# A Mamba-style block with a gated feed-forward: first batch's opening spread over other engines, and the batch loop written out

## The chip, the core and the metric

The kernel runs on one core of a Trainium2 chip. Its engines work side by side, each from its own instruction queue: TensorE (PE; its weight loads are shown as PEld), VectorE (DVE), ScalarE (ACT), GpSimd (POOL), and SyncE (SP), which here only issues DMA transfers. They are ordered by semaphores alone. The metric is the device time of one execution in microseconds, the median of several runs; lower is better.

## The reference

Input x is 4 x 512 x 512 (batch, position, channel), all in fp32. With D = 1024, N = 16, R = 32:

```python
xn = (x - mean) / sqrt(var + 1e-5)
u, gate = split(xn @ W_in.T)                     # 1024 each
u = silu(causal_conv4(u) + conv_b)               # depthwise, along the positions
dt, Bm, Cm = split(u @ Wx.T, [32, 48])           # 32, 16, 16
dt, Bm, Cm = rmsnorm(dt)*w1, rmsnorm(Bm)*w2, rmsnorm(Cm)*w3
delta = softplus(dt @ Wdt.T + dt_bias)
# for every position t:
state = exp(delta_t * A) * state + (delta_t * u_t) * B_t
y_t = sum_n state * C_t
s = ((y + u * D_param) * silu(gate)) @ W_out.T
ffn = (silu(xn @ w_gate.T) * (xn @ w_up.T)) @ w_down.T   # inner width 1376
out = x + s * silu(ffn)
```

## The kernel before

Channels lie on the 128 partitions and the 512 positions along a row, so the recurrence over positions is VectorE's scan instruction on a 128 x 512 tile, one for each of 8 channel tiles and 16 states: 128 scans a batch, in 64 slots of two. A slot s of a batch is: ScalarE makes two decay tiles `exp(delta * A)` in the PSUM banks `dA[0]`, `dA[1]` (L598); GpSimd makes the input pair `dBu = v * B` with v = delta * u, 128 x 1024, in one of three buffers (L814); VectorE scans twice (L1041); TensorE transposes the states into the banks `hT` (L1391); and VectorE (L970, L961), or ScalarE with GpSimd (L694, L784), adds them times C to `yT`. Around that, in every slot, each engine has further steps written out by slot number (`side(s)`): the feed-forward of the same batch, whose weight products are TensorE's largest work, and the opening of the next batch (normalisation, u, gate, delta). Matmuls on x are done in three products of high and low parts (`from_x`, L1102, 12 matmuls for a tile); the low part of a weight entry is the rest that GpSimd takes (`rest_w`, L750) after ScalarE's rounding (`round_w`, L463). Entries come through a ring of two.

The first batch has no batch before it, so its opening stands ahead of all slots:

- SyncE loads x in four tiles and the first weight entries (two at once, each later one when GpSimd has taken the rest of the one two before). ScalarE's queue issues the identity and seven constants (L444, L445); semaphore `const_in` counts the seven.
- VectorE takes `bn_stats` of the four tiles (L878). GpSimd's `power_ln` (L719 to L736) turns them to scale and shift in eleven small steps of 4 columns, one the power -0.5 (L732). ScalarE normalises (L459), TensorE transposes, ScalarE and VectorE split x in high and low (L453, L882). Ahead of that VectorE waits for all constants and halves two of them (L933, L934).
- u in 8 tiles: TensorE; ScalarE's first tap (L492); VectorE's three taps (L892); ScalarE's tanh (L499) and "+1" (L503); GpSimd's product (L755). Then TensorE's small matmuls with Wx (L1107), two groups of four for each u tile.
- ScalarE squares, VectorE sums rows (L903, L904), GpSimd's `power_rms` scales, adds and takes the power over 12 columns (L741 to L745), ScalarE scales rows (L518, L519); dt and B are transposed, B goes out to DRAM and comes back row by row, spread over the partitions (`bb`).
- delta in two pairs of tiles: TensorE (L1120), ScalarE's exponentials (L581) and logarithms (L548), for which it loads another function table, VectorE's clamp (L945), GpSimd's v (L766). Then ScalarE loads the first table again (for tanh, L552), takes the second of the first four gate tiles and the C rows (L526), VectorE copies C (L909) and makes the products of gate tiles 0 and 1 (L913). Gate tiles 2 and 3 wait on TensorE for the banks of 0 and 1.
- Slot 1's ScalarE part ends with the rounding of the first feed-forward entry, which needs all four gate tiles; GpSimd takes its rest in slot 2, and TensorE's feed-forward starts on it.

`sequences` runs the body of a batch for batch 0, for batches 1 and 2 in a hardware loop with the batch number in a register, and for batch 3.

## Time and profile before

| | |
|---|---|
| median of 3 runs | 1177.55 us (1175.94 to 1177.86) |
| the profiled execution | 1172.87 us, span 1171.1 us |
| TensorE busy | 1062.0 us, 91% |
| VectorE busy | 1035.4 us, 88% |
| GpSimd busy | 998.4 us, 85% |
| ScalarE busy | 702.6 us, 60% |
| granted TensorE clock, mean | 0.968 of full |

The span goes from the first to the last instruction of the profiled execution; its own time has 1.8 us around it. Busy shares are means over stages that have different limits, so they do not tell what an edit is worth; the waits at the place of the edit do. A granted clock of 1.0 is 2.4 GHz, of 0.5 it is 1.2 GHz.

### The profile page before, as it was taken

Reading aid. Unit: us, or ns where it says so; the run is one execution under the profiler, and the core shown is the slowest. Engines: PE = TensorE matmul, PEld = TensorE weight load, DVE = VectorE, ACT = ScalarE, POOL = GpSimd, SP = SyncE. Lnnn points to the kernel's source line nnn. Section 1 sums busy time; section 2 is a strip of 40 time slices with the busy share of each in tenths; the row PEclk is TensorE's granted clock in tenths of the full one; section 3 lists DMA queues with packets and bytes.
Section 4 is the critical chain, followed back from the end, with each engine's and each line's share of the span. In section 5 each row is a group of like instructions: output and inputs, shape, how many; then the busy total and the mean of one; then the engine's idle time right before and its main releaser. Section 6 shows DMA issues by size and latency. Waiting matters only on the chain.

```text
span 1171.1 us, 16696 instructions
## 1 busy us (share of the span) xinstructions
PE 1062.0 (91%) x5072; PEld 757.3 (65%) x5072; DVE 1035.4 (88%) x1232; ACT 702.6 (60%) x1140; POOL 998.4 (85%) x572
## 2 busy tenths in 40 slices
PE   5979988889989999989997999998998999999767
PEld 4757766666658776666756786576756787555444
DVE  4469999999989999899987999899998999888895
ACT  4656646866665756677573766476576665465440
POOL 3678899899988899789987899879989889879961
PEclk9969999899999999999998999999999999999878
DMA  4636754534333544343323453334233353325310
GB/s 129 215 107 225 233 193 142 171 118 135 101 98 137 209 144 161 127 153 100 115 76 128 153 208 145 117 135 153 89 111 118 135 181 108 126 99 180 117 63 37
DMA packets 46567, 160.83 MB, mean 137 GB/s; under 512 B 5355, under 2 KB 5611, under 8 KB 37004
## 3 DMA queue, kind: packets, MB, share of 16 engines
q1 hardware_dynamic: 45424, 159.14, 39.6%
q8 instruction: 44, 0.72, 0.2%
q10 hardware_dynamic: 1052, 0.59, 0.2%
q14 instruction: 47, 0.39, 0.1%
HBM read 135.33 MB, written 24.38 MB: 136 GB/s over the span
## 4 chain that ended last, share of the span: by engine, by line
PE 52%; DVE 20%; issue 12%; POOL 11%; ACT 4%; DVEq 1%; DMA 0%; SPq 0%; POOLq 0%; ACTq 0%
PE pj L1102 18%; PE hT L1391 11%; DVE sb_h L1041 10%; PE pj L1300 7%; POOL sb_dBu L814 5%; DVE sb_yT L970 5%; PE pj L1334 5%; PE pj L1365 3%; PE pj L1120 2%; DVE sb_un L892 2%; PE pj L1409 2%; PE pj L1107 2%; POOL sb_yT L784 2%; POOL sb_un L755 1%; POOL sb_v L766 1%
## 5 line engine op out<-in xcount | busy, mean ns | idle before, releaser
L814 POOL TENSOR_TENSOR sb_dBu<-sb_v,sb_bb 128x1024 f32<-128x1024 f32 x256 | 607.1, 2385 | 28.5 <-DVE sb_h L1041 20.0
L1041 DVE TENSOR_TENSOR_SCAN sb_h<-dA,sb_dBu 128x512 f32<-128x512 f32 x512 | 597.9, 1212 | 29.0 <-POOL sb_dBu L814 17.0
L598 ACT ACTIVATE dA<-sb_delta,sb_apar 128x512 f32<-128x512 f32 x512 | 345.7, 688 | 246.1 <-DVE sb_h L1041 242.4
L1102 PE MATMUL pj<-sb_x_hi,sb_w_sp 128*128 128x512 f32 x1208 | 344.3, 409 | 21.8 <-DVE sb_un L892 12.0
L1391 PE MATMUL hT<-sb_ident,sb_h 128*128 128x128 f32 x2048 | 287.3, 282 | 63.8 <-DVE sb_yT L970 50.3
L1391 PEld LDWEIGHTS hT<-sb_ident,sb_h 128*128 128x128 f32 x2048 | 242.3, 144 | 148.6 <-issue 50.2
L970 DVE SCALAR_TENSOR_TENSOR sb_yT<-hT,sb_cs,sb_yT 128x512 f32<-128x512 f32 x335 | 239.3, 740 | 43.8 <-PE hT L1391 43.2
L1102 PEld LDWEIGHTS pj<-sb_x_hi,sb_w_sp 128*128 128x128 f32 x1208 | 220.6, 192 | 84.6 <-issue 24.3
L784 POOL TENSOR_TENSOR sb_yT<-sb_yT,sb_part 128x512 f32<-128x512 f32 x141 | 181.2, 1285 | 57.6 <-ACT sb_part L694 57.4
L694 ACT ACTIVATE sb_part<-hT,sb_cs_act 128x512 f32<-128x512 f32 x141 | 96.4, 684 | 139.6 <-PE hT L1391 138.0
L1102 PE MATMUL pj<-sb_x_lo,sb_w_sp 128*128 128x512 f32 x604 | 167.1, 400 | 0.0
L1102 PEld LDWEIGHTS pj<-sb_x_lo,sb_w_sp 128*128 128x128 f32 x604 | 116.2, 192 | 27.1
L1334 PE MATMUL pj<-sb_S,sb_ring 128*128 128x512 f32 x264 | 121.8, 599 | 0.0
L1300 PE MATMUL pj<-sb_u,sb_ring 128*128 128x512 f32 x192 | 86.6, 594 | 0.0
L1334 PEld LDWEIGHTS pj<-sb_S,sb_ring 128*128 128x128 f32 x264 | 46.9, 190 | 52.6 <-issue 52.6
L892 DVE SCALAR_TENSOR_TENSOR sb_un<-pj,sb_cw,sb_un 128x511 f32<-128x511 f32 (+2 forms) x93 | 69.5, 748 | 4.8 <-ACT sb_un L492 2.6
L750 POOL TENSOR_TENSOR sb_w_sp<-sb_ring,sb_w_sp 128x1024 fp32r<-128x1024 f32 x21 | 50.0, 2382 | 27.0 <-ACT sb_w_sp L463 26.9
L1300 PEld LDWEIGHTS pj<-sb_u,sb_ring 128*128 128x128 f32 x192 | 34.6, 190 | 34.9 <-issue 34.6
L770 POOL TENSOR_TENSOR sb_u<-sb_u,sb_sgate 128x512 f32<-128x512 f32 x32 | 41.2, 1293 | 11.3 <-DVE sb_u L919 11.3
L766 POOL TENSOR_TENSOR sb_v<-sb_delta,sb_un 128x1024 f32<-128x1024 f32 x16 | 38.3, 2392 | 8.9 <-DVE sb_delta L945 8.5
L761 POOL TENSOR_TENSOR sb_delta<-sb_delta,sb_v 128x1024 f32<-128x1024 f32 x14 | 33.5, 2390 | 11.1 <-ACT sb_v L548 11.1
L755 POOL TENSOR_TENSOR sb_un<-sb_v,sb_un 128x512 f32<-128x512 f32 x32 | 41.1, 1291 | 0.0
(126 smaller groups left out, 800.0 us busy)
## 6 DMA issues: line engine op xcount, KB each, us to landing
sb_w_sp<-w_cache SPq DMA_DIRECT2D x55, 1024.0 KB, 4.8
sb_ring<-w_ring SPq DMA_DIRECT2D x67, 512.0 KB, 3.4
sb_bb<-b_rows SPq DMA_DIRECT2D x128, 256.0 KB, 3.6
w_cache<-sb_w_sp SPq DMA_DIRECT2D x19, 1024.0 KB, 4.9
sb_xio<-x SPq DMA_DIRECT2D x7, 1024.0 KB, 8.0
out<-sb_xio SPq DMA_DIRECT2D x3, 1024.0 KB, 5.7
sb_xio<-x SPq DMA_DIRECT2D x4, 256.0 KB, 3.5
out<-sb_xio SPq DMA_DIRECT2D x4, 256.0 KB, 2.0
```

What stands on the lines that cost most here:

```text
L598: nc.scalar.activation(dA[g % 2][:, :], delta[:, j, :], ACT.Exp, scale=apar[:, j, n:n + 1]).then_inc(dA_done, 1)
L694: nc.scalar.activation(dst, hT[c % H_BANKS][:, :], ACT.Copy, scale=cs_act[:, c, n:n + 1]).then_inc(ev_done, 1)
L755: nc.gpsimd.tensor_tensor(un[:, j, :], cth[:, j % 2, :], un[:, j, :], ALU.mult).then_inc(u_done, 1)
L784: nc.gpsimd.tensor_tensor(y, y, part[:, (len(acts) - q) % 2, :], ALU.add).then_inc(yp_done, 1)
L814: nc.gpsimd.tensor_tensor(dBu[:, dbu_buffer(s), :, :], v[:, j:j + 2, :], bb[:, i % B_RING, :].unsqueeze(1).to_broadcast([P, 2, T]), ALU.mu ...
L892: nc.vector.scalar_tensor_tensor(out=acc[:, k:T], in0=bank[:, 0:T - k], scalar=cw[:, j, KC - 1 - k:KC - k], in1=acc[:, k:T], op0=ALU.mult, ...
L970: nc.vector.scalar_tensor_tensor(out=y, in0=hT[c % H_BANKS][:, :], scalar=cn, in1=y, op0=ALU.mult, op1=ALU.add).then_inc(y_done, 1)
L1041: nc.vector.tensor_tensor_scan(h[:, i % 2, 2 * part + e, :], dA[g % 2][:, :], dBu[:, dbu_buffer(s), e, :], 0.0, ALU.mult, ALU.add).then_in ...
L1102: done = nc.tensor.matmul(bank[:, :], w[:, kk * P:(kk + 1) * P], xs[:, kk, :], start=(p == 0), stop=(p == len(products) - 1))
L1300: done = nc.tensor.matmul(pj[e % 2][:, :], ring[:, slot_of(b, OUT0 + e), part, m * P:(m + 1) * P], u[:, j, :], start=(j == 0), stop=(j == ...
L1334: done = nc.tensor.matmul(pj[DOWN_BANK[e]][:, :], ring[:, slot_of(b, DOWN0 + x3 // 2), x3 % 2, t % 4 * P:(t % 4 + 1) * P], S[:, t, :], sta ...
L1391: done = nc.tensor.transpose(hT[c % H_BANKS][:, j * P:(j + 1) * P], h[:, i % 2, j, c * P:(c + 1) * P], ident[:, :])
```

## The change

- **Constants.** The seven constant transfers move from ScalarE's queue to SyncE's, between the first and the second weight entry.
- **Layer statistics.** VectorE does the small steps (the sum of means is scaled by an immediate, scale and shift are reordered so that the doubling falls away); GpSimd keeps the power alone.
- **u.** For the last two of eight tiles VectorE does "+1" and product in one instruction; ScalarE's "+1" and GpSimd's product fall away.
- **RMS.** VectorE does scale and add; GpSimd's power is split in one over eight columns (dt and B) and one over four (C), each with its own count, so that `rms_done` has two counts for batch 0.
- **v and dBu of slots 0 and 1** are made by VectorE, in `first_pair`, behind the clamp of their pair, with a semaphore of their own (`dBu_first`); counts of `dBu_done` are two lower from there on (`pairs_made`).
- **Decays of slot 0** come on ScalarE ahead of the second pair's logarithms. Its second gate tanh and the C rows move into slot 0's side work; VectorE's first gate product moves ahead of the pairs, the second into slot 0, the copy of C into slot 1.
- **The loop.** `sequences` is a Python loop over four batches, so all of them are written out with constant counts.

```diff
@@ -325,14 +326,16 @@
...
+        def pairs_made(b, s):
+
+            return dBu_done, b * SLOTS + s - 2
+
...
-        def sequences(eng, body):
-            body(0, True, False)
-            with eng.Fori(1, NB - 1) as b:
-                body(b, False, False)
-            body(NB - 1, False, True)
+        def sequences(body):
+            for b in range(NB):
+                body(b, b == 0, b == NB - 1)
@@ -356,6 +359,10 @@
...
                 load(p % W_RING, (FIRST + RING_FIRST)[p])
+                if p == 0:
+                    for dst, src in consts:
+                        sp.dma_start(dst[:], src).then_inc(const_in, 16)
+                    sp.dma_start(lnw[:, :], ln_w.partition_broadcast(P)).then_inc(const_in, 16)
@@ -407,7 +414,10 @@
...
                     if what == "row":
-                        sp.wait_ge(dBu_done, b * SLOTS + 2 * k + 2)
+                        if first and k == 0:
+                            sp.wait_ge(dBu_first, 2)
+                        else:
+                            sp.wait_ge(*pairs_made(b, 2 * k + 2))
@@ -440,9 +450,6 @@
...
             act.dma_start(ident[:, :], ident_d).then_inc(id_in, 16)
-            for dst, src in consts:
-                act.dma_start(dst[:], src).then_inc(const_in, 16)
-            act.dma_start(lnw[:, :], ln_w.partition_broadcast(P)).then_inc(const_in, 16)
@@ -512,7 +519,7 @@
...
-                act.wait_ge(rms_done, c + 1)
+                act.wait_ge(rms_done, 1 if isinstance(c, int) and c == 0 else c + 2)
@@ -559,6 +566,7 @@
...
             act.wait_ge(half_done, 2)
+            act.wait_ge(init_done, N_INIT)
@@ -566,8 +574,8 @@
...
                     conv_tanh(0, j - 1)
-                    conv_plus1(0, j - 1)
-            act.wait_ge(init_done, N_INIT)
+                    if j - 1 < KD - 2:
+                        conv_plus1(0, j - 1)
@@ -579,11 +587,13 @@
...
                     nc.scalar.activation(delta[:, j, :], first_z_bank[j][:, :], ACT.Exp).then_inc(ze_done, 1)
+                if p == 1:
+
+                    act.wait_ge(del_done, 1)
+                    for e in range(2):
+                        nc.scalar.activation(dA[e][:, :], delta[:, e, :], ACT.Exp, scale=apar[:, e, 0:1]).then_inc(dA_done, 1)
...
                     softplus_log(0, j, delta)
-            gate_tanh(0, 1, pj[1])
-
-            take_c(0)
@@ -601,6 +611,10 @@
...
                 def side(s):
+                    if first and s == 0:
+                        gate_tanh(0, 1, pj[1])
+                        act.wait_ge(rms_done, 2)
+                        take_c(0)
@@ -612,7 +626,7 @@
...
                         if j == JH and not first:
-                            act.wait_ge(dBu_done, b * SLOTS)
+                            act.wait_ge(*pairs_made(b, 0))
@@ -694,7 +708,8 @@
...
                 for s in range(SLOTS):
-                    decay(s)
+                    if not (first and s == 0):
+                        decay(s)
@@ -751,7 +766,8 @@
...
             def conv_silu(c, j):
-                pool.wait_ge(th1_done, c * KD + j + 1)
+
+                pool.wait_ge(th1_done, c * KD + j + 1 if isinstance(c, int) and c == 0 else c * KD + j - 1)
@@ -783,16 +799,21 @@
...
-            power_ln(0)
+            pool.wait_ge(ln_var, 1)
+            nc.gpsimd.tensor_tensor(rstd[:, 1, :], rstd[:, 0, :], half[:, 0:TC], ALU.pow).then_inc(ln_rstd, 1)
...
                     rest_w(p % W_RING, p % HI_RING, p + 1)
-                conv_silu(0, j)
-            power_rms(0)
-            inputs(0, 0)
+                if j < KD - 2:
+                    conv_silu(0, j)
+
+            pool.wait_ge(mse_done, 2)
+            nc.gpsimd.tensor_tensor(ms[:, 2, :, 0:2], ms[:, 1, :, 0:2], half[:, 0:2 * TC].rearrange("p (c g) -> p c g", g=2),
+                                    ALU.pow).then_inc(rms_done, 1)
+            nc.gpsimd.tensor_tensor(ms[:, 2, :, 2:3], ms[:, 1, :, 2:3], half[:, 0:TC].unsqueeze(2), ALU.pow).then_inc(rms_done, 1)
@@ -805,6 +826,11 @@
...
                             pool.wait_ge(out_dma, b * 16)
+                    if first and s < 2:
+
+                        continue
+                    if first and s < 4:
+                        pool.wait_ge(v_done, s - 1)
@@ -814,8 +840,6 @@
...
                                             ALU.mult).then_inc(dBu_done, 1)
-                    if s == 0 and first:
-                        inputs(b, 1)
@@ -929,6 +953,19 @@
...
                 ln_stats(0, t)
+            dve.wait_ge(ln_stat, TC)
+            nc.vector.tensor_tensor(mv[:, 0, :], stats[:, :, 1], stats[:, :, 4], ALU.add).then_inc(ln_aggr, 1)
+            nc.vector.tensor_tensor(mv[:, 1, :], stats[:, :, 1], stats[:, :, 4], ALU.subtract).then_inc(ln_aggr, 1)
+            nc.vector.tensor_tensor(mv[:, 2, :], stats[:, :, 2], stats[:, :, 5], ALU.add).then_inc(ln_aggr, 1)
+            dve.wait_ge(ln_aggr, 3)
+            nc.vector.tensor_scalar(mv[:, 0, :], mv[:, 0, :], -0.5, None, ALU.mult).then_inc(ln_aggr, 1)
+            nc.vector.tensor_tensor(mv[:, 1, :], mv[:, 1, :], mv[:, 1, :], ALU.mult).then_inc(ln_aggr, 1)
+            nc.vector.tensor_scalar(mv[:, 2, :], mv[:, 2, :], 1.0 / H, LN_EPS, ALU.mult, ALU.add).then_inc(ln_aggr, 1)
+            dve.wait_ge(ln_aggr, 6)
+            nc.vector.scalar_tensor_tensor(out=rstd[:, 0, :], in0=mv[:, 1, :], scalar=0.25, in1=mv[:, 2, :],
+                                           op0=ALU.mult, op1=ALU.add).then_inc(ln_var, 3)
+            dve.wait_ge(ln_rstd, 1)
+            nc.vector.tensor_tensor(rstd[:, 2, :], mv[:, 0, :], rstd[:, 1, :], ALU.mult).then_inc(ln_rstd, 1)
@@ -937,18 +974,35 @@
...
                 taps(0, j, first_u_bank[j])
+            for j in (KD - 2, KD - 1):
+                dve.wait_ge(th_done, j + 1)
+                dve.wait_ge(u_done, j)
+                nc.vector.scalar_tensor_tensor(out=un[:, j, :], in0=cth[:, j % 2, :], scalar=1.0, in1=un[:, j, :],
+                                               op0=ALU.add, op1=ALU.mult).then_inc(u_done, 1)
             rms_squares(0)
+            dve.wait_ge(ms_done, 2)
+            nc.vector.tensor_scalar(ms[:, 1, :, 0:1], ms[:, 0, :, 0:1], 1.0 / R, RMS_EPS, ALU.mult, ALU.add).then_inc(mse_done, 1)
+            nc.vector.tensor_scalar(ms[:, 1, :, 1:3], ms[:, 0, :, 1:3], 1.0 / N, RMS_EPS, ALU.mult, ALU.add).then_inc(mse_done, 1)
...
                 weigh(slice(t, t + 1), first_ssm_bank[t][:, 0:F].unsqueeze(1))
-            for j in range(JH):
-                dve.wait_ge(sp_done, j + 1)
-                step = nc.vector.scalar_tensor_tensor(out=delta[:, j, :], in0=delta[:, j, :], scalar=Z_MAX, in1=first_z_bank[j][:, :],
-                                                      op0=ALU.min, op1=ALU.max)
-                if j % 2 == 1:
-                    step.then_inc(del_done, 1)
-            hand_c(0)
-            for j in range(2):
-                gate_silu(0, j, pj[j])
+            gate_silu(0, 0, pj[0])
+
+            def first_pair(p):
+                pair = slice(2 * p, 2 * p + 2)
+                for j in (2 * p, 2 * p + 1):
+                    dve.wait_ge(sp_done, j + 1)
+                    step = nc.vector.scalar_tensor_tensor(out=delta[:, j, :], in0=delta[:, j, :], scalar=Z_MAX, in1=first_z_bank[j][:, :],
+                                                          op0=ALU.min, op1=ALU.max)
+                step.then_inc(del_done, 1)
+                dve.wait_ge(del_done, p + 1)
+                nc.vector.tensor_tensor(v[:, pair, :], delta[:, pair, :], un[:, pair, :], ALU.mult).then_inc(v_done, 1)
+                if p == 0:
+                    dve.wait_ge(b_in[0], 16)
+                dve.wait_ge(v_done, p + 1)
+                nc.vector.tensor_tensor(dBu[:, dbu_buffer(p), :, :], v[:, pair, :], bb[:, 0, :].unsqueeze(1).to_broadcast([P, 2, T]),
+                                        ALU.mult).then_inc(dBu_first, 1)
+
+            first_pair(0)
@@ -973,6 +1027,10 @@
...
                 def side(s):
+                    if first and s == 0:
+                        gate_silu(0, 1, pj[1])
+                    if first and s == 1:
+                        hand_c(0)
@@ -1034,7 +1092,12 @@
...
                     i, part = s // 2, s % 2
-                    dve.wait_ge(dBu_done, b * SLOTS + s + 1)
+                    if first and s < 2:
+                        if s == 1:
+                            first_pair(1)
+                        dve.wait_ge(dBu_first, s + 1)
+                    else:
+                        dve.wait_ge(*pairs_made(b, s + 1))
```

(Lines that only pass the changed arguments of `sequences` are left out.)

## Rows read from the trace of the kernel before

**Rows 1.** The page, chain that ended last: share of the span by engine.
```profile
PE 52%; DVE 20%; issue 12%; POOL 11%; ACT 4%; DVEq 1%; DMA 0%; SPq 0%; POOLq 0%; ACTq 0%
```
**Rows 2.** Timeline, start: start us, us, engine, line, operation, out<-in, count [idle before <-releaser].
```profile
4.41 0.99 ACTq L445 DMA_DIRECT2D sb_lnw<-ln_w  x1
...
5.40 0.69 DVE L878 BATCH_NORM_STATS2 sb_stats<-sb_xio 128x6 f32<-128x512 f32 x1 [0.24 <-DMA sb_xio<-x]
...
7.81 0.69 DVE L878 BATCH_NORM_STATS2 sb_stats<-sb_xio 128x6 f32<-128x512 f32 x1 [1.71 <-DMA sb_xio<-x]
...
10.38 1.02 POOL L732 TENSOR_TENSOR sb_rstd<-sb_mv,sb_half 128x4 f32<-128x4 f32 x1
...
11.63 0.18 DVE L933 TENSOR_SCALAR sb_cw<-sb_cw 128x32 f32<-128x32 f32 x1 [3.12 <-DMA sb_lnw<-ln_w]
...
12.00 2.93 ACT L459 ACTIVATE sb_xio<-sb_xio,sb_rstd 128x512 f32<-128x512 f32 x4 [5.29 <-POOL sb_rstd L736]
...
17.32 2.48 DVE L882 TENSOR_TENSOR sb_x_lo<-pj,sb_x_hi 128x512 fp32r<-128x512 f32 x4 [5.44 <-ACT sb_x_hi L453]
```
**Rows 3.** Timeline, end of the stage that makes u.
```profile
41.01 2.32 DVE L892 SCALAR_TENSOR_TENSOR sb_un<-pj,sb_cw,sb_un 128x511 f32<-128x511 f32 x3 [0.32 <-ACT sb_un L492]
...
44.31 2.48 POOL L755 TENSOR_TENSOR sb_un<-sb_v,sb_un 128x512 f32<-128x512 f32 x2
...
44.85 0.61 PE L1107 MATMUL dA<-sb_wx,sb_un 128*128 128x64 f32 x4
...
47.34 0.61 PE L1107 MATMUL dA<-sb_wx,sb_un 128*128 128x64 f32 x4
```
**Rows 4.** Timeline, row sums of squares to their powers.
```profile
49.67 0.21 POOL L741 TENSOR_TENSOR sb_ms<-sb_ms,sb_per 128x12 f32<-128x12 f32 x1 [2.88 <-DVE sb_ms L904]
...
50.26 2.27 POOL L745 TENSOR_TENSOR sb_ms<-sb_ms,sb_half 128x12 f32<-128x12 f32 x1
```
**Rows 5.** Timeline, softplus to the first slots.
```profile
61.01 2.34 POOL L766 TENSOR_TENSOR sb_v<-sb_delta,sb_un 128x1024 f32<-128x1024 f32 x1 [8.47 <-DVE sb_delta L945]
...
63.56 1.28 ACT L552 ACT_TABLE_LOAD   x1
...
66.26 1.30 ACT L598 ACTIVATE dA<-sb_delta,sb_apar 128x512 f32<-128x512 f32 x2
...
66.40 1.27 DVE L913 SCALAR_TENSOR_TENSOR sb_sgate<-sb_sgate,pj 128x512 f32<-128x512 f32 x2
...
74.98 0.60 ACT L552 ACTIVATE sb_sgate<-pj 128x512 f32<-128x512 f32 x1 [0.93 <-PE pj L1102]
...
81.35 2.34 DVE L1041 TENSOR_TENSOR_SCAN sb_h<-dA,sb_dBu 128x512 f32<-128x512 f32 x2
```
**Rows 6.** The chain in order of time: start us, us, engine, tile, line, count.
```profile
21.12 19.05 PE pj L1102 x84
...
79.00 5.49 PE pj L1102 x12
...
625.87 4.33 issue
...
631.31 4.41 PE pj L1102 x12
...
637.03 2.75 PE pj L1102 x12
```
**Rows 7.** Timeline: first scan of batches 1 to 3, third step-size addition of 2, 3.
```profile
346.78 1.23 DVE L1041 TENSOR_TENSOR_SCAN sb_h<-dA,sb_dBu 128x512 f32<-128x512 f32 x1 [2.54 <-POOL sb_dBu L814]
...
617.79 1.22 DVE L1041 TENSOR_TENSOR_SCAN sb_h<-dA,sb_dBu 128x512 f32<-128x512 f32 x1 [2.61 <-POOL sb_dBu L814]
...
677.93 2.38 POOL L761 TENSOR_TENSOR sb_delta<-sb_delta,sb_v 128x1024 f32<-128x1024 f32 x1
...
894.64 1.22 DVE L1041 TENSOR_TENSOR_SCAN sb_h<-dA,sb_dBu 128x512 f32<-128x512 f32 x1 [2.52 <-POOL sb_dBu L814]
...
948.59 2.38 POOL L761 TENSOR_TENSOR sb_delta<-sb_delta,sb_v 128x1024 f32<-128x1024 f32 x1
```

More of the change, by code:

```diff
@@ L259, in build @@
         dA_done = sem("dA_done")
+        dBu_first = sem("dBu_first")
         dBu_done = sem("dBu_done")
@@ L432, in sequence @@
                         sp.dma_start(xio[:, :, :], rows(x, b)).then_inc(xr_in, 16)
-            sequences(sp, sequence)
+            sequences(sequence)
             for c in range(TC):
@@ L708, in sequence @@
                         round_entry(b, *HI_AT[s])
-            sequences(act, sequence)
+            sequences(sequence)
         @block.gpsimd
@@ L851, in sequence @@
                         inputs(b + 1, s - SLOTS + 2)
-            sequences(pool, sequence)
+            sequences(sequence)
             for m, c in OFF_ADDS[False]:
@@ L1048, in sequence @@
                     side(s)
-            sequences(dve, sequence)
+            sequences(sequence)
             b = NB - 1
@@ L1411, in tail_out @@
                     done.then_inc(tail_ps, 1)
-            sequences(pe, sequence)
+            sequences(sequence)
             b = NB - 1
```

## The prediction

> **What bounds the kernel now.** I read the chain that ended last first [rows 1]: TensorE holds 52% of it, VectorE 20%, GpSimd 11%, and 12% is "issue", time in which an engine waited for nothing that the profile shows. No single engine is the limit of the whole; each stage has its own, and a stage that is passed earlier moves everything behind it, since nothing in the kernel is tied to absolute time. So I then read the timeline of the first 90 us, where the change works, and last the joints between the batches, where the loop is taken away.
>
> In the first 12 us nothing but small work stands between the last tile of x and ScalarE's normalisation: VectorE waits 1.71 us for that tile, takes its statistics from 7.81 to 8.50, GpSimd works until ScalarE starts at 12.00 [rows 2]. Then TensorE is the limit for seven u tiles, in one unbroken piece of the chain up to 40.17 [rows 6]. The end of u's stage is set by GpSimd again: its last two products run from 44.31 to 46.79 and TensorE's last small matmuls end at 47.95 [rows 3]. Next comes the RMS power on GpSimd [rows 4], and then the stretch from the softplus to the first feed-forward matmuls at 79.00, in which all engines wait for each other in turn [rows 5, 6].
>
> **The change, part by part.**
>
> *Arrival of x.* Seven constant transfers leave ScalarE's queue, where the last was issued at 4.41 and so shared the DMA engines with x, and stand on SyncE's behind the fourth x tile and the first weight entry. VectorE was free at 5.40 + 0.69 = 6.09 and waited to 7.81 [rows 2]. Upper bound of the gain: both waits, 1.71 + 0.24, so 2.0; lower bound nothing, if the tile waits for other tiles of its own queue. I take 1.7, the last wait, since x is then alone on the engines but for the identity. The price stands elsewhere: seven issues (the last took 0.99 [rows 2], the others about half, so 4 us) come before the second weight entry, which is then issued at about 7.1. ScalarE rounds it only after the four normalisations (2.93 from 12.00, so from 9.2 after the change) and the first rounding, at some 13. VectorE's queue stands still for the constants too; behind them are the halvings and the rests of x, first needed 5.3 us after ScalarE's start (17.32 less 12.00) [rows 2]. The last constant came 7.2 us after its issue began (11.63 less 4.41); from 6.1 that is 13.3, against 14.5 needed. Both are covered by 1 us or more, and what exceeds that is lost one for one.
>
> *Layer statistics.* GpSimd took 3.50 us from 8.50 to 12.00, of it 1.02 for the power [rows 2]. The small steps go to VectorE, whose small steps follow each other at 0.09 us when independent and last 0.18 [rows 2]: three (0.36), three (0.36), one (0.18), a hand-over and the power (1.2), a hand-over and the product (0.25): 2.35, a gain of 1.1. Bounds: 0.6 if every VectorE step waits its full length and the hand-overs double, 1.4 at best.
>
> *u.* VectorE ends its taps at 43.33 and can do both last products at once: 0.66 to 0.75 each, where GpSimd, held by a rest, started at 44.31 and needed 1.24 each [rows 3]. But TensorE's twelfth of sixteen groups of small matmuls ends at 45.46, 5.3 us after 40.17, so 0.44 each, and it cannot end before 47.3; it ended at 47.95. Gain 0.65, bounds 0.3 and 0.7. ScalarE's two dropped "+1" steps lay beside other work.
>
> *RMS.* GpSimd's two scalings, 49.67 to 50.26, become VectorE steps with one hand-over (gain about 0.3), and the power over twelve elements, 2.27, becomes one over eight that is waited for, and one over four behind it. Four cost 1.02, twelve 2.27, so eight about 1.65: 0.6 less. Gain 0.9 [rows 2, 4]; bounds 0.3 (power costs the same whatever its size) and 1.2.
>
> *Decays, dBu, gates.* Times here are those of before, without the 4.35 us that are won up to here. Before: logarithms up to the table load at 63.56, this to 64.84, gate step, C rows, two decays, and both gate products from 66.40 to 67.67; only these free TensorE's banks, and TensorE ends the last two gate tiles when ScalarE takes the last at 74.98; then a rounding, GpSimd's rest, and the feed-forward starts at 79.00: a block of 4.0 us behind the last gate tile [rows 5, 6]. After: two decays (1.30 [rows 5]) go in front of the logarithms, so the table is there at 66.15 and the second gate step ends at 66.75, VectorE's product at 67.45. The first bank was freed long before, at about 51, so TensorE does gate tile 2 beside the softplus and only tile 3 is left: 2.75 at full clock [rows 6], end 70.25, not 74.98. Gain on TensorE's side 4.7; if the clock is low there, the same 12 matmuls cost 4.4 to 5.5 [rows 6] and the gain is about 2.
>
> VectorE pays for this: v and dBu of two pairs. No row has this shape on VectorE. From below twice its 512-wide step with two inputs, 1.27 [rows 5]; from above GpSimd's 2.34 for the same shape. I take 1.28, the same lanes and twice the elements. First pair: from 60.95, when delta is ready (GpSimd took it up at 61.01), to 63.5; decays are there at 63.1 and 63.8; scans to 65.9, so the gate product at 66.75 finds VectorE free. Second pair 67.45 + 3 x 1.28 = 71.3, two scans to 73.65, C rows and a gate product to 74.5; slot 3, which comes after slot 2's two scans, two additions and a gate product (4.4), stands at 78.9, not 81.35 (-2.45). So TensorE -4.7, VectorE -2.45 at first; TensorE's first feed-forward tile took 5.49 at low clock before, and a tile at 2.75 would let VectorE's next slots close up. The chain runs over TensorE from 79.00 [rows 6], so I go towards its side: 4.1, bounds 2.0 and 4.7.
>
> The Trainium skill, SBUF — State Buffer, section "Who interferes with whom", says that a VectorE instruction with two SBUF inputs and a GpSimd instruction that reads SBUF exclude each other for a whole instruction, whichever starts first. No row here has VectorE with two such inputs beside a GpSimd product, so the trace neither confirms nor denies it. What it would make of the time is the first rival below.
>
> *No loop.* Batches 1 and 2 run the same instructions. Batch 1, first scan to first scan, lasts 617.79 - 346.78 = 271.01, batch 2 894.64 - 617.79 = 276.85, 5.84 more. Batch 3 has the same work as batch 2 up to GpSimd's third step-size addition, and is entered without a jump: there it is 948.59 - 894.64 = 53.95 after its first scan, batch 2 677.93 - 617.79 = 60.14, 6.2 more [rows 7]. Batch 2 alone is entered by the jump back. In the chain it has 4.33 us of "issue" between two groups of TensorE transposes, and then 12 matmuls of 4.41 instead of 2.75 [rows 6]: 4.33 + 1.66 = 6.0, the whole difference, and the batch's length shows that it is not made up later. With all batches written out the jump is gone. Register arithmetic would show as more than 6.0 of difference to batch 3, and does not beyond 0.2. I take 5.9; bounds 4.3 and 6.2.
>
> **Sum.** 1.7 + 1.1 + 0.65 + 0.9 + 4.1 + 5.9 = 14.35. The profiled execution took 1172.87 (span 1171.1), so 1158.5 for one like it; the median of the runs is 1177.55, 4.7 above, and gives 1163.2. Forecast 1163.
>
> **Rivals.**
> *VectorE's new products and GpSimd's exclude each other.* GpSimd's third dBu (2.34) becomes ready at the same moment as VectorE's first, 62.2. If it starts first, VectorE's runs from 64.6, the scans end at 68.15, the gate product is 1.4 late and with it tile 3: 1164.6. For it: the same operands release both. Against: VectorE takes up a ready instruction some 0.05 sooner. 0.11.
> *The constants come late,* or the second weight entry behind them: the 2.8 of the start are lost, 1166.0. For it: the last constant came 7.2 us after its issue. Against: then x and both entries were in its way. 0.08.
> *The jump is not the cause* and TensorE stalls in batch 2 as before: 1169.1. For it: only one jump to look at. Against: batch 3's start and batch 1's length. 0.10.
> *The low clock vanishes* in more stretches (79.0's tile at 5.49 among them), since TensorE waits less: up to 5 more, 1158. 0.06.
> *Slower: each written-out batch stalls at its start* for its code as batch 2 does now. Three starts at 5.9 instead of one are +11.8, less 8.45: +3.4, 1180.9. It decides from 4.8 per start (8.45 + 5.9 over three). Against: batches 1 and 3 start on code that is run for the first time, without a stall [rows 7]. 0.05.
> The forecast has 0.60.
>
> **Numbers.** Bounds of the terms added up: 0 + 0.6 + 0.3 + 0.3 + 2.0 + 4.3 = 7.5 and 2.0 + 1.4 + 0.7 + 1.2 + 4.7 + 6.2 = 16.2, so 1170 and 1161; with the clock's rival below it the range is 1157 to 1170, which leaves out the slower rival and little more. A change under 0.2% (2.4 us) can't be told from none. Faster 0.93, same 0.02, slower 0.05.
>
> **What would show it.** After: ScalarE's first normalisation near 9.2, its RMS scaling near 48.1, first scan near 59.2 (63.5 less 4.35), feed-forward start near 70, 8 to 9 earlier than 79.0; no "issue" of over 1 us in TensorE at the start of batch 2; batches 1 and 2 equal in length to 1 us. Wrong if ScalarE's second rounding or VectorE's halvings end their idle time with a DMA, if gate tile 3 runs at low clock, or if a written-out batch shows TensorE waiting for "issue".

## The result, and the profile after

The changed kernel took 1163.53 us (median of 4 runs, 1156.73 to 1165.08), the kernel before, run beside it, 1176.74 (4 runs, 1173.49 to 1177.86): a ratio of 0.9893, 95% interval [0.9866, 0.992]. A second measurement of both (below, changed_again) gave 0.9892 [0.9874, 0.9911]. The forecast was 1163. The profiled execution has a span of 1160.5, against 1171.1 before: 10.5 less in the profiles, 12 to 13 less in the medians.

The page's chain by engine, of the changed kernel. TensorE stands at 46% against 52% in [rows 1]. These 6 points are no measure of the change: the share is 45 to 46% in nine of the changed kernel's relatives below and 55% in two, others_loop and opening_only.
```profile
PE 46%; DVE 22%; POOL 15%; issue 11%; ACT 6%; DMA 0%; SPq 0%; DVEq 0%; POOLq 0%; ACTq 0%
```
The timeline of its start (start us, us, engine, line, operation, out<-in, count [idle before <-releaser]), to read beside [rows 2]:
```profile
5.44 1.50 DVE L902 BATCH_NORM_STATS2 sb_stats<-sb_xio 128x6 f32<-128x512 f32 x2 [0.45 <-DMA sb_xio<-x]
...
8.07 1.02 POOL L803 TENSOR_TENSOR sb_rstd<-sb_rstd,sb_half 128x4 f32<-128x4 f32 x1 [7.63 <-DVE sb_rstd L965]
9.13 0.16 DVE L968 TENSOR_TENSOR sb_rstd<-sb_mv,sb_rstd 128x4 f32<-128x4 f32 x1 [1.21 <-POOL sb_rstd L803]
9.32 0.81 ACT L466 ACTIVATE sb_xio<-sb_xio,sb_rstd 128x512 f32<-128x512 f32 x1 [6.87 <-DVE sb_rstd L968]
9.84 0.18 DVE L970 TENSOR_SCALAR sb_cw<-sb_cw 128x32 f32<-128x32 f32 x1 [0.55 <-DMA sb_lnw<-ln_w]
```
The statistics no longer wait long for x, one power is left on GpSimd, and ScalarE normalises at 9.32 (9.2 forecast). The constants do end VectorE's idle time (0.55 us), which the forecast had named as a sign of being wrong. Here it cost nothing: the halvings run at 9.84, and what stands behind them, the rests of x, is first taken at 14.64.

The end of u's stage and the RMS power, for [rows 3, 4], on VectorE, GpSimd and TensorE:
```profile
40.57 2.55 DVE L980 SCALAR_TENSOR_TENSOR sb_un<-sb_v,sb_un 128x512 f32<-128x512 f32 x2
45.47 0.29 DVE L927 TENSOR_REDUCE sb_ms<-sb_nrm 128x4 f32<-128x128 f32 x1 [2.35 <-ACT sb_nrm L514]
...
39.41 2.36 POOL L765 TENSOR_TENSOR sb_w_sp<-sb_ring,sb_w_sp 128x1024 fp32r<-128x1024 f32 x1 [0.63 <-ACT sb_w_sp L470]
46.31 1.64 POOL L814 TENSOR_TENSOR sb_ms<-sb_ms,sb_half 128x8 f32<-128x8 f32 x1 [4.54 <-DVE sb_ms L985]
...
47.98 0.32 ACT L525 ACTIVATE sb_nrm<-sb_ssm,sb_ms 128x32 f32<-128x32 f32 x1
```
Eight elements of the power took 1.64 (1.65 forecast), ScalarE's scaling stands at 47.98 (48.1 forecast). The first of these rows holds a surprise: VectorE's two products took 2.55 us, where 0.66 to 0.75 each was expected. GpSimd's rest ran until 39.41 + 2.36 = 41.77. The first product took 1.75 and ended at 42.32, 0.55 behind the rest; the second, alone, took 0.69. So the first stood still for some 1.06 us beside GpSimd's rest. It cost nothing here, since the small matmuls were the limit.

The first slots on VectorE, for [rows 5], and behind them the two GpSimd and TensorE rows that matter:
```profile
56.28 1.23 DVE L998 TENSOR_TENSOR sb_v<-sb_delta,sb_un 128x1024 f32<-128x1024 f32 x1
57.61 1.23 DVE L1002 TENSOR_TENSOR sb_dBu<-sb_v,sb_bb 128x1024 f32<-128x1024 f32 x1
58.87 2.34 DVE L1104 TENSOR_TENSOR_SCAN sb_h<-dA,sb_dBu 128x512 f32<-128x512 f32 x2
61.38 0.69 DVE L937 SCALAR_TENSOR_TENSOR sb_sgate<-sb_sgate,pj 128x512 f32<-128x512 f32 x1 [0.18 <-ACT sb_sgate L559]
...
57.77 3.30 POOL L840 TENSOR_TENSOR sb_dBu<-sb_v,sb_bb 128x1024 f32<-128x1024 f32 x1 [8.85 <-DMA sb_bb<-b_rows]
...
62.12 1.20 PE L1165 MATMUL pj<-sb_x_hi,sb_w_sp 128*128 128x512 f32 x4 [0.48 <-DVE sb_sgate L937]
...
69.89 1.86 PE L1165 MATMUL pj<-sb_x_hi,sb_w_sp 128*128 128x512 f32 x4
```
v and dBu took 1.23 each on VectorE (1.28 forecast), the first scan stands at 58.87 (59.2), gate tile 3 starts at 62.12 at full clock, and the feed-forward at 69.89 (near 70). GpSimd's own dBu beside them took 3.30 instead of 2.34.

The four batches, first scan to first scan and the last one to the end: 282.24, 270.73, 270.71, 278.00, before 279.19, 271.01, 276.85, 276.43. Batches 1 and 2 are now equal, as forecast. Batch 0 grew by 3.05. Its first scan stands 8.7 us earlier than before and its slot 16 11.2 us earlier (127.7 against 138.9), but batch 1's first scan only 5.7: half of the lead of slot 16 is lost again. The windows of slots 44 to 54 show where (us, then busy us and count of TensorE, its weight loads, VectorE, ScalarE and GpSimd, granted clock, DMA share, GB/s):
```profile
252.00:276.00 24.00, 21.65 (x106) 14.81 (x105) 22.85 (x27) 16.20 (x27) 24.00 (x17) 1.00 0.48 165
276.00:290.00 14.00, 14.00 (x66) 13.71 (x66) 7.88 (x9) 3.71 (x7) 12.92 (x7) 0.51 0.15 39
290.00:300.00 10.00, 10.00 (x53) 7.56 (x52) 8.81 (x13) 6.33 (x16) 6.53 (x6) 1.00 0.27 105
```
From 276.2 to 289.9 TensorE's granted clock was half (0.51 of 2.4 GHz, so its level of 1.2), though it had been busy 21.65 of the 24 us before. It was never idle in these 14 us, and VectorE was busy for 7.88 of them. Slot 50 starts at 276.0. In the kernel before it starts at 288.1, and there the clock stayed full, though TensorE had been busy for 21.54 of the 24 us ahead, as good as the same. What became slow are TensorE's small matmuls with Wx for the next batch, here in the changed kernel and in opening_only (below), which was spared:
```profile
280.13 6.93 PE L1170 MATMUL pj<-sb_wx,sb_un 128*128 128x64 f32 x32
...
278.27 3.68 PE L1176 MATMUL pj<-sb_wx,sb_un 128*128 128x64 f32 x32
```

### The profile page after: what moved, and what is told of

Same layout as the page of the kernel before. It is cut to its first block, busy times and chain, and to the rows that moved or that the text cites. A ratio compares the mean times of both kernels' runs of the same rounds, so it can differ in the third digit from the quotient of the medians.

```text
span 1160.5 us, 14932 instructions
## 1 busy us (share of the span) xinstructions
PE 1065.1 (92%) x5072; PEld 760.4 (66%) x5072; DVE 1043.5 (90%) x1248; ACT 701.9 (60%) x1138; POOL 985.8 (85%) x555
## 4 chain that ended last, share of the span: by engine, by line
PE 46%; DVE 22%; POOL 15%; issue 11%; ACT 6%; DMA 0%; SPq 0%; DVEq 0%; POOLq 0%; ACTq 0%
PE pj L1165 13%; DVE sb_h L1104 12%; PE hT L1454 9%; PE pj L1363 7%; POOL sb_dBu L840 7%; DVE sb_yT L1024 5%; PE pj L1397 4%; PE pj L1428 3%; PE pj L1183 3%; POOL sb_yT L800 3%; PE pj L1170 2%; PE pj L1472 2%; DVE sb_un L916 2%; POOL sb_un L771 1%; ACT dA L608 1%
## 5 line engine op out<-in xcount | busy, mean ns | idle before, releaser
L1454 PE MATMUL hT<-sb_ident,sb_h 128*128 128x128 f32 x2048 | 290.4, 284 | 60.0 <-DVE sb_yT L1024 49.1
L1454 PEld LDWEIGHTS hT<-sb_ident,sb_h 128*128 128x128 f32 x2048 | 244.8, 146 | 144.8 <-issue 49.8
L1165 PE MATMUL pj<-sb_x_lo,sb_w_sp 128*128 128x512 f32 x604 | 163.9, 393 | 0.0
L1428 PE MATMUL pj<-sb_ring,sb_S 128*128 128x512 f32 x88 | 39.8, 592 | 0.0
L771 POOL TENSOR_TENSOR sb_un<-sb_v,sb_un 128x512 f32<-128x512 f32 x30 | 38.6, 1290 | 0.0
```

The lines of the kernel that those rows point to most:

```text
L1165: done = nc.tensor.matmul(bank[:, :], w[:, kk * P:(kk + 1) * P], xs[:, kk, :], start=(p == 0), stop=(p == len(products) - 1))
L1428: done = nc.tensor.matmul(pj[c][:, :], S[:, t, c * P:(c + 1) * P], ring[:, slot_of(b, q), t % 2, :], start=(t == 0), stop=(t == KI - 1))
L1454: done = nc.tensor.transpose(hT[c % H_BANKS][:, j * P:(j + 1) * P], h[:, i % 2, j, c * P:(c + 1) * P], ident[:, :])
```

## Experiments

Ratios are to the kernel before, measured beside each kernel; in brackets is the 95% interval. No ratio here differs from 1 by as much as 2%, and most of these kernels differ from each other by less than their intervals, so the parts of the change are read from the traces, one execution of each.

**loop_only**: the kernel before, the batches written out.
```diff
-            body(0, True, False)
-            with eng.Fori(1, NB - 1) as b:
-                body(b, False, False)
-            body(NB - 1, False, True)
+            for b in range(NB):
+                body(b, b == 0, b == NB - 1)
```


> The kernel before with nothing but the batch loop written out. If the jump back is what stalls TensorE, batch 2 (first scan to first scan) falls from 276.85 to about 271.0 us, the 4.33 us of issue at TensorE's start of batch 2 is gone, and the time is 5.9 us under the kernel before. If the stall comes from something else at that place, batch 2 stays near 276.9 and the time within 1 us. If a written-out batch stalls for its code at each start, every batch shows 4 us or more of issue there and the time rises by about 12.

Measured: 1169.46 (7 runs), ratio 0.9939 [0.9917, 0.996], so 7.2 us, with 4.7 to 9.8 by the interval (the medians differ by 6.5). Batches 279.08, 270.69, 270.72, last 279.65. Batch 2 lost its 6 us, and no batch got a stall of its own.

**opening_only**: the changed kernel with the loop put back on all five engines (the diff above, reversed).

> The changed kernel with the hardware loop put back on all five engines. If the two halves of the change add up, the first batch is as in the changed kernel (first scan at 58.9, feed-forward start at 69.9), batch 2 is 5.9 us longer than batch 1, and the time is 5 to 6 us above the changed kernel, about 8 to 11 us under the kernel before as far as the low clock in the first batch allows.

Measured: 1166.72 (6 runs), ratio 0.9933 [0.9906, 0.996], 7.9 us. Batch 2 is 278.70 again, against 270.97 for batch 1: 7.7 longer, where 5.9 was expected. The two halves of the change cannot be told apart in size, and their sum, 15.1, is above the 11.7 to 13.2 of the whole by no more than their intervals allow.

**pe_loop** and **others_loop**: the loop only in TensorE's program, and only in the other four.
```diff
-            sequences(sequence)
+            sequences(sequence, pe)
```
The second argument is the engine that gets its `Fori` back; the lines shown are those of pe_loop.

> The changed kernel with the loop put back on TensorE's queue alone; the other four engines keep straight code. If it is TensorE's own jump that costs, all of it comes back: about 4.3 us of issue at TensorE's start of batch 2 and a batch 2 that is 5.9 us longer than batch 1. If the jumps of the other engines cost as well, less than 4 us comes back.

> The changed kernel with the loop put back on the other four engines, TensorE straight. By the theory that TensorE's jump is the cause batches 1 and 2 are equal to 0.5 us and the time is that of the changed kernel. By the rival (any engine's jump stalls the joint) batch 2 is 2 us or more longer than batch 1.

Measured: pe_loop 1166.27 (4 runs), 0.9918 [0.9888, 0.9947], batches 1 and 2 270.65 and 277.64. others_loop 1162.47 (4 runs), 0.9884 [0.9851, 0.9918], 271.01 and 270.88. The chain of pe_loop at the start of batch 2 (start us, us, what):
```profile
619.25 0.65 PE hT L1460 x4
619.90 5.11 issue
625.02 1.11 PE hT L1460 x4
626.13 3.98 PE pj L1171 x12
```
That is the picture of [rows 6], 5.11 of "issue" and then twelve matmuls at 3.98 instead of 2.75. In others_loop TensorE waits there for VectorE only, 1.76 us at most, and never for "issue". The jump back that costs is TensorE's alone. Its price is not the same each time: batch 2 is 5.8 us longer than batch 1 in the kernel before (4.33 of "issue"), 7.0 in pe_loop (5.11) and 7.7 in opening_only (5.38, and then 5.03 for the twelve matmuls).

**middle_before**: of the changed kernel, v and dBu of the first two pairs back on GpSimd, decays behind the logarithms, C rows and second gate step at their old places; everything else as changed.
```diff
...
-                if p == 1:
-                    act.wait_ge(del_done, 1)
-                    for e in range(2):
-                        nc.scalar.activation(dA[e][:, :], delta[:, e, :], ACT.Exp, ...)
...
+            gate_tanh(0, 1, pj[1])
+            act.wait_ge(rms_done, 2)
+            take_c(0)
```


> The changed kernel with decays, v, dBu and gate steps of the first slots arranged as in the kernel before (decays of slot 0 behind the logarithms and the table load, v and dBu on GpSimd, both gate products at the end). If my term for this part (4.1 us) is right, the feed-forward starts 4 to 5 us later after the first layer normalisation than in the changed kernel (60.6 us after it there), slot 16 lies 4 to 6 us later, and the time is 4 to 6 us above the changed kernel. If a rival is right that this part is taken up by later slots anyway, slot 16 lies under 2 us later.

**pairs_pool**: only v and dBu of the first two pairs back on GpSimd.

> The changed kernel with only v and dBu of slots 0 and 1 back on GpSimd (2.34 us each instead of 1.23 on VectorE); early decays and early gate product stay. If what counts in this part is TensorE's gate tile 2 running beside the softplus, TensorE's feed-forward start moves by under 1.5 us and slot 16 by under 2. If VectorE's quicker pairs are the gain, slots 0 to 3 are 2 us or more later and slot 16 follows them.

Measured: middle_before 1162.35 (5 runs), 0.9892 [0.9864, 0.9919]; pairs_pool 1165.44 (7 runs), 0.9918 [0.9893, 0.9942]. In the whole time, the middle part cannot be told from nothing. What it does must be read in the traces, below. There middle_before lies under what was expected of it (feed-forward 4 to 5 us later than in the changed kernel, slot 16 4 to 6, both behind the first normalisation): the feed-forward starts 3.0 us later, 63.6 against 60.6, and slot 16 2.3 (120.7 against 118.4).

In pairs_pool slot 16 is 6.3 us later than in the changed kernel (124.7), which is 4.0 more than in middle_before. This is no price of GpSimd's products alone. The clamp of the second pair stayed in slot 1, behind the first scans and a gate product, and GpSimd's v waits for it. The second clamp in pairs_pool, and in middle_before:
```profile
64.36 1.28 DVE L989 SCALAR_TENSOR_TENSOR sb_delta<-sb_delta,pj 128x512 f32<-128x512 f32 x2
...
58.36 1.28 DVE L981 SCALAR_TENSOR_TENSOR sb_delta<-sb_delta,pj 128x512 f32<-128x512 f32 x2 [1.35 <-ACT sb_delta L552]
```
So middle_before is the kernel to compare with.

**consts_act**: the seven constants back on ScalarE's queue. **stats_pool**: the small steps of the layer statistics back on GpSimd.
```diff
-                    for dst, src in consts:
-                        sp.dma_start(dst[:], src).then_inc(const_in, 16)
...
+            for dst, src in consts:
+                act.dma_start(dst[:], src).then_inc(const_in, 16)
...
```


> The changed kernel with the seven constants back on ScalarE's queue. If they were what held the fourth tile of x, its statistics start at 7.2 to 7.8 us instead of 5.9 to 6.6 and the first normalisation at 10.7 to 11.0 instead of 9.0 to 9.7; the last constant then lands after VectorE's small steps. If the tile waits for its own queue alone, the statistics start no later than 6.6.

> The changed kernel with all small steps of the first layer statistics back on GpSimd. From the end of the fourth statistics to the first normalisation 3.50 us as before, instead of 2.4: 1.1 us later from there on. If hand-overs between VectorE and GpSimd eat the gain, under 0.5 us.

Measured: consts_act 1164.68 (4 runs), 0.9898 [0.9865, 0.9931]; stats_pool 1165.26 (4 runs), 0.9902 [0.9863, 0.9941]. Both are too small to show in the time. In the traces stats_pool shows clearly; consts_act shows too, by one trace and a narrow margin. The fourth tile's statistics start at 7.20 in consts_act, 7.81 and 7.18 in the kernel before and loop_only; in the eleven other traces between 5.86 and 7.01, 6.4 in the mean. Its first normalisation, expected at 10.7 to 11.0, is at 10.28. From there to the first normalisation it is 4.19 or 4.20 in stats_pool, loop_only and the kernel before, 3.07 or 3.08 wherever VectorE has the steps.

**changed_again**: the changed kernel a second time.

> The changed kernel, unchanged. Theory (the clock, granted differently from execution to execution, moves single stages by up to 6 us; the change itself is worth about 12): median 1163, within 2 us; in the profile the low stretches in the first 290 us stand at other places than in the first execution, and the seventeenth scan group (slot 16) lies 118 to 124 us behind the first normalisation (118.4 in the first execution) while the steps that do not depend on TensorE (first RMS reduce at 36.2 behind the normalisation) stay within 0.2. Rival (the opening's extra gain is the program's own, not the clock's): slot 16 again at 118.4 within 0.5, and the low stretches at the same places.

Measured: 1162.9 (5 runs), 0.9892 [0.9874, 0.9911]. The theory fell: low clock stood at the same places as in the first trace, within 0.1 us (54.2 for 6.8, 67.9 for 3.4, 187.4 for 17.1, 276.1 for 13.7), and slot 16 at 118.24 behind the first normalisation against 118.38. In two executions of this kernel chance did not strew the clock over this stretch. Something seems to decide it, and so I went back to the traces that differ. VectorE's and GpSimd's first dBu, in changed_again:
```profile
57.37 1.23 DVE L1002 TENSOR_TENSOR sb_dBu<-sb_v,sb_bb 128x1024 f32<-128x1024 f32 x1
...
57.51 3.31 POOL L840 TENSOR_TENSOR sb_dBu<-sb_v,sb_bb 128x1024 f32<-128x1024 f32 x1 [8.82 <-DMA sb_bb<-b_rows]
```
and in pe_loop, whose opening is the same code:
```profile
58.00 3.43 DVE L1008 TENSOR_TENSOR sb_dBu<-sb_v,sb_bb 128x1024 f32<-128x1024 f32 x1
61.47 2.34 DVE L1110 TENSOR_TENSOR_SCAN sb_h<-dA,sb_dBu 128x512 f32<-128x512 f32 x2
63.73 0.66 DVE L943 SCALAR_TENSOR_TENSOR sb_sgate<-sb_sgate,pj 128x512 f32<-128x512 f32 x1
...
57.98 2.38 POOL L846 TENSOR_TENSOR sb_dBu<-sb_v,sb_bb 128x1024 f32<-128x1024 f32 x1 [8.66 <-DVE sb_v L1004]
...
64.44 1.29 PE L1171 MATMUL pj<-sb_x_hi,sb_w_sp 128*128 128x512 f32 x4 [2.54 <-DVE sb_sgate L943]
```
Whoever starts first keeps its own time, and the other is held. Where GpSimd's operands (its part of the B rows comes by DMA) are there before v is, both engines are released by v together, GpSimd starts 0.02 to 0.03 us sooner, and VectorE's dBu takes 3.43 instead of 1.23. Where the B rows come a little after v, GpSimd starts 0.06 to 0.16 us behind VectorE, and VectorE loses nothing.

The eleven traces up to here, by my arithmetic on their start times (us; low clock: length of the stretches at half clock that reach into slots 2 to 5):
```
                 first dBu on VectorE   slot 3 after the     slot 3 to   low clock,
                 (held: over 3 us)      first RMS reduce     slot 16     slots 2 to 5
before           on GpSimd              32.24                57.55       6.8 us
loop_only        on GpSimd              32.77                57.53       6.8
pairs_pool       on GpSimd              31.91                56.62       6.8
middle_before    on GpSimd              29.78                54.77       none
pe_loop          3.43, held             29.59                57.43       6.8
others_loop      3.43, held             29.58                57.44       6.8
consts_act       3.43, held             29.55                57.52       6.8
stats_pool       3.44, held             29.60                57.28       6.8
changed          1.23                   27.44                54.79       3.4, early
changed_again    1.23                   27.27                54.82       3.4, early
opening_only     1.23                   27.15                54.80       3.4, early
```
Two steps stand out: 2.2 us in slot 3 with the held dBu, and 2.65 us between slots 3 and 16 with low clock in the first feed-forward tiles. In pe_loop TensorE waits 2.54 us for gate tile 3 and 1.41 for the next weights, in others_loop 2.66 and 1.40, and both have low clock around these waits. In the lower three it waits 0.48, 0.32 and 1.81 for gate tile 3, runs that at full clock, and has its clock back before or within the second third of the first feed-forward tile.

The mark is the RMS reduce and not the normalisation, because the stretch between the two moves by itself: 36.2 us in seven of the nine traces of this table that have the changed u and RMS stages, 37.2 and 37.3 in the two others, others_loop and consts_act. The difference arises in TensorE's first u tile, which took 4.6 us there and 3.5 in the changed kernel.

**warm_opening**, **warm_early**, **early_gate**: is the clock a cause of its own, and can the order of the gate steps be bettered? Their expectations were written before the table above.
```diff
             transpose_dt(0, dA[0])
+            for q in range(6):
+                nc.tensor.transpose(dA[1][:, 0:P], ident[:, :], ident[:, :])
...
-            pe.wait_ge(del_done, 1)
+            pe.wait_ge(del_done, 2)
+            for q in range(28):
+                nc.tensor.transpose(pj[3][:, 0:P], ident[:, :], ident[:, :])
```


> The changed kernel with TensorE given work that nobody uses while it would wait in the opening: 6 transposes of the identity (about 0.3 to 0.5 us each) into the second dA bank behind the transposes of dt, and 28 (8 to 12 us) into gate tile 3's bank once the last softplus batch is done; the output is unchanged. Theory (gate tiles 2 and 3 and the first feed-forward tiles run at low clock only because TensorE waited before them, and that costs time behind them): gate tile 2 or the first feed-forward tiles show 2.75 to 3.3 us a tile instead of 4.4 to 5.5, slot 16 at 118.4 or earlier behind the first normalisation; time 1160 to 1162. Rival 1 (VectorE fills the same time, the clock there is worth nothing): low stretches gone and slot 16 unchanged, time as the changed kernel within 1 us. Rival 2 (the added transposes stand in front of real matmuls): feed-forward start over 1 us later behind the first normalisation than in the changed kernel (60.5), time 1 to 4 us above it.

The second gate step moved ahead, alone in early_gate and with the transposes in warm_early (the table load of the logarithms then stands behind the copy of dt):
```diff
-            nc.scalar.preload_act_table_set("natural_log_exp_and_others")
+            gate_tanh(0, 1, pj[1])
             hand_dt(0, dA[0])
+            nc.scalar.preload_act_table_set("natural_log_exp_and_others")
```


> As warm_opening, and the first pair's second gate step (tanh on ScalarE, product on VectorE) stands ahead of the softplus's logarithms, so that TensorE can start gate tile 3 earlier. Theory (after the change the second gate step still holds gate tile 3): feed-forward starts 1 to 3 us earlier than in warm_opening, and the first scan 1 us later; time 0 to 2 us under warm_opening. Rival (VectorE's scans set the end of the opening): the first scan's delay is passed on to slot 16, time 0 to 2 us over warm_opening.

> The changed kernel with only the second gate step ahead of the softplus. Theory (VectorE's side sets the opening): slot 3 to slot 16 behind the first normalisation as in the changed kernel or up to 1.5 us later, time within 2 us of it. Rival (TensorE's side sets it): gate tile 3 and the feed-forward start 1 to 3 us earlier and slot 16 with them, time 1 to 3 us under it.

Measured: warm_opening 1162.36 (6 runs), 0.9888 [0.9865, 0.991]; warm_early 1159.99 (5 runs), 0.9874 [0.9853, 0.9895]; early_gate 1162.81 (5 runs), 0.9895 [0.9878, 0.9912]. None is to be told from the changed kernel; warm_early has the lowest median, but its interval overlaps those of the other two and of both measurements of the changed kernel. The theory of warm_opening did not come true: the low clock in slots 2 to 5 is gone, but slot 16 is at 120.1 behind the normalisation and not at 118.4, and the feed-forward starts at 61.6, 1.0 later. Ahead of the RMS reduce 1.2 of that were lost, in TensorE's first u tile; from the reduce to slot 16 it is 82.8 against 82.2. The 28 transposes took 3.2 us (4.9 in warm_early, partly at low clock), not 8 to 12, so they filled less than was planned.

In warm_early VectorE's dBu was held (3.44), and yet slots 3 to 16 took 54.76, with full clock from 61.8 behind the normalisation on. So the 2.65 us do not come from the held dBu as such. They stand in the traces that have 6.8 us of low clock in slots 2 to 5 (56.6 to 57.6 us for slots 3 to 16), and in none of the others: 54.8 in all seven traces with 3.4 or none there. That a held dBu brings the low clock on by TensorE's wait is the likely reading, not shown: warm_early moved the gate step and added the transposes at once, and is one execution. In early_gate and warm_opening the B rows came so late that VectorE itself waited for them (1.43 and 0.85), which the chain of early_gate shows, DMA in it for the first time:
```profile
52.36 3.68 DMA b_rows<-sb_dtB
56.04 0.02 issue
56.06 3.44 DMA sb_bb<-b_rows
59.50 0.02 issue
59.52 1.24 DVE sb_dBu L1003
```
Moving the gate step forward leaves no wait before gate tile 3, but the feed-forward starts 1.4 us later behind the normalisation than in the changed kernel (62.0), not earlier, and slot 3 is at 27.89 after the RMS reduce: less the wait of 1.43 for the B rows that is 26.5, about the 0.7 of the gate product less that VectorE had in its way. From dBu to the transposes ahead of the feed-forward this chain runs over VectorE alone, which is the limit here.

## Why the prediction was right, and which terms were not

*Arrival of x, 1.7*: too large. Mean against mean (7.4 in the three traces with the constants on ScalarE's queue, 6.4 in the others) it is 1.0. The wait did not vanish: VectorE still waits 0.45 us for the third tile and 0.11 for the fourth in the changed kernel, and the fourth tile's arrival moves by 1.1 us from execution to execution, so one trace's wait of 1.71 was no measure of it.

*Layer statistics, 1.1*: 4.19 less 3.08, 1.11. Right. *u, 0.65*: from the end of the last u tile to that of the small matmuls 7.09 (44.58 less 37.49), before 7.78: 0.69. Right, in spite of the 2.55 us products. *RMS, 0.9*: from the first reduce to the first scaling 2.51 against 3.44, 0.93; another 0.28 lies between the last small matmul and the reduce, which the forecast did not have.

*Decays, dBu, gates, 4.1*: the step that failed is "so I go towards its side". On the clock of the trace TensorE's side was forecast well: feed-forward at 69.89. But against middle_before it starts only 3.0 earlier, not 4.7, and the forecast's gain was measured against a first tile at low clock before, 5.49 us, which middle_before has at 3.4 without the edit (1.21, 1.09 and 1.08 for its thirds). Against middle_before, VectorE's slot 3 is 2.3 to 2.6 us earlier, slot 16 by the same, and this is VectorE's term of 2.45, carried on unchanged. It holds only where VectorE's dBu goes first. Where it is held, slot 3 gains 0.2 and, with the low clock behind it, slot 16 is 2.3 to 2.5 later behind the RMS reduce than in middle_before (the four held traces of the table).

*First rival, products exclude each other (0.11)*: its mechanism is real, and the forecast took the wrong side of the coin toss. "VectorE takes up a ready instruction some 0.05 sooner" was wrong: GpSimd was 0.02 to 0.03 us sooner, in all five traces in which v released both. What saved the profiled execution was not the take-up but B rows so late that GpSimd started 0.16 us behind. The rival's price for the held dBu (2.34) was right, 2.20 was measured; its effect on the gate product was set at 1.4 and is 2.0 to 2.2, and 2.65 at low clock stand behind it. The Trainium skill, SBUF — State Buffer, section "Who interferes with whom", states this very thing, for a VectorE instruction with two SBUF inputs beside a GpSimd instruction, whichever starts first. The traces agree three times: 3.43 for 1.23 on VectorE, 3.30 for 2.34 on GpSimd, 2.55 for two u products of 0.69.

*No loop, 5.9*: batch 2 is 6.14 shorter, in loop_only, changed_again and others_loop too (276.85 to between 270.68 and 270.88). Right, and pe_loop with others_loop shows that it is TensorE's jump. The rival of a stall in every batch and that of a jump without blame both fell.

*The sum.* With the measured terms it is 1.0 + 1.1 + 0.7 + 1.2 + 2.4 + 6.0 = 12.4, against 14.35 forecast and 13.2 and 11.7 in the two measurements of the medians. That is less of a proof than it looks, because what stands outside the terms cancels. In the profiled executions, before to changed, the first normalisation comes 2.7 us earlier (12.00 to 9.32). From there to slot 16 it is 8.5 us less (126.9 to 118.4): 0.7 of u, 1.2 of RMS, 2.3 of the middle, and 4.3 that middle_before has as well, without the middle's edits. Of these 4.3, 2.8 lie between slots 3 and 16, with 6.8 us of low clock before and none in middle_before, and 1.5 ahead of slot 3; no run shows what brings them. From slot 16 to batch 1 5.5 us are lost again, the last batch is 1.6 longer, the loop gives 6.1 and batch 1 0.3: 10.5 in all, the difference of the two spans.

The forecast came out at 1163 and not 1165 because it was made from a median of 1177.55, and the kernel before ran at 1176.74 and 1174.56 beside it, so 0.8 to 3 us lower. So the hit is partly luck: terms that were 2 too large met a base that was too high by about as much.

*The clock's rival (0.06)* foresaw less low clock; what came is a trade. The mean granted clock is 0.968 in both profiled executions. The low clock in slots 2 to 5 is down from 6.8 to 3.4 us, and a stretch of 13.7 us at slots 50 to 52 is new. From slot 16 to batch 1's first scan the changed kernel, changed_again and the three last experiments take 213.4 to 213.6 us, the kernel before, middle_before and six others 207.1 to 207.9. Its price is about 6 us (from slot 47 to slot 55 it is 37.6 us in the changed kernel, 31.9 before), which is why middle_before, 2.4 behind at slot 16, is no slower in the end. The five traces with it all have 17.1 us of low clock at slots 29 to 33, where the others have two shorter stretches; stats_pool, with 6.8 us of it, takes 210.2. What grants this stretch is open: opening_only has the changed kernel's code and times up to slot 30 (118.11 at slot 16), and was spared. No run was made that moves it alone.

That one order of GpSimd and VectorE or the other is taken in a share of all executions, and so makes part of the spread of the medians, is argued: only one execution of each kernel has a trace. Holding GpSimd's third dBu back until VectorE's first is done would fix the order; it was not tried, and what it costs is not known. Where VectorE went first, GpSimd's product ended at 61.07 (changed kernel) against 60.36 in pe_loop, and then GpSimd stood idle for 5.72 us.

## What to carry to other kernels

When work is moved from GpSimd to VectorE, look at which GpSimd product the same semaphore releases: here a tie of 0.02 us decided over 2.2. An explicit order would take the luck out; no run here tried it. Compare an edit with a kernel that differs in nothing else, and stage by stage from a common mark; a gain read against one execution with low clock in it counts the clock as the edit's. Where a loop runs twice, price TensorE's jump back (here 6 to 8 us) before anything smaller.

## What the hardware showed that was not expected

- GpSimd's power costs about by the element: 1.02 us for 4 columns, 1.64 for 8, 2.27 for 12 [rows 2, 4].
- A VectorE product of 128x1024 with two SBUF inputs takes 1.23 us, GpSimd's 2.34 to 2.39. The one that starts second is held: VectorE's took 3.43 when GpSimd was 0.02 ahead, GpSimd's 3.30 when VectorE was 0.16 ahead.
- Four engines jump back without a cost in the chain, TensorE with 4.3 to 5.4 us of "issue" and 1.2 to 2.3 of low clock behind it.
- TensorE's granted clock fell to half for 13.7 us after 24 us in which it was busy for 21.65, and stayed full in the kernel before after 21.54. Fewer waits early did not keep it up later.
